# A two-layer graph kernel: the second product with U21 moved into the first step, diffusion tiles and exponentials put ahead of each group's first transposes

## The reference, cut to what matters

```python
h = maximum(layernorm(x), 0);  x = x + L0(h, adj)        # quantised support, then adj @ support
X = maximum(layernorm(x), 0)
R = (S + I) / rowsum(S + I);  Z = 0;  Xf = Xa = X        # S is adj
for s in range(2):
    A = adj_from_feats(Xa, W1, W2, W3)   # softmax(Xa W1 W2 (Xa W3)^T), the top 0.9 kept, softmax again
    Xf = R @ Xf
    Xa = A @ Xa
    Z = Z + (Xf @ U1s[s] + Xa @ U2s[s])
Y = X + Z
return x + (layernorm(Y) * gamma + beta)
```

## Time and profile before

| | |
|---|---|
| median of 3 runs | 1463.36 us (1462.64 to 1469.3) |
| the profiled execution | 1465.6 us, its span 1463.8 us |
| layer 0, up to the first logits of step 0 | 0 to 353.2 us |
| step 0, up to the first logits of step 1 | 353.2 to 923.8 us |
| step 1 with the output | 923.8 to 1463.8 us |
| busy, share of the span | TensorE 85%, VectorE 76%, ScalarE 41%, GpSimd 20% |
| mean granted TensorE clock | 0.967 |

### The profile page before, as it was taken

How to read it: one execution, slowest core, us unless ns; L and a number is a source line. 1 busy time by engine, 2 the same in 40 slices (tenths; PEclk the granted TensorE clock), 3 DMA queues, 4 the chain that set the end, 5 groups by cost and what they waited for, 6 DMA issues and landing times.

```text
span 1463.8 us, 18743 instructions
## 1 busy us (share of the span) xinstructions
PE 1239.3 (85%) x6458; PEld 607.9 (42%) x6458; DVE 1113.8 (76%) x1880; ACT 600.1 (41%) x1129; POOL 291.1 (20%) x233
## 2 busy tenths in 40 slices
PE   0348999997699689999989899789799999999994
PEld 0123555553244245444545454234344444444442
DVE  6985777773699999269949900499899989879667
ACT  1332444444831244455454343760234364353331
POOL 3312343432122213011122111011101011011011
PEclk9888999999899899999999999989999999999998
DMA  6124455442134211121110140524421121120244
GB/s 209 57 86 169 178 190 188 179 161 90 44 118 143 86 49 66 42 75 51 37 65 30 32 157 30 194 72 146 127 66 58 37 94 43 38 72 30 97 153 175
DMA packets 57687, 143.95 MB, mean 98 GB/s; under 512 B 9664, under 2 KB 9664, under 8 KB 53248
## 3 DMA queue, kind: packets, MB, share of 16 engines
q1 hardware_dynamic: 57600, 142.91, 28.3%
HBM read 90.72 MB, written 52.17 MB: 98 GB/s over the span
## 4 chain that ended last, share of the span: by engine, by line
PE 63%; issue 15%; ACT 9%; DVE 6%; POOL 4%; DMA 4%; POOLq 0%; SPq 0%; DVEq 0%; ACTq 0%
PE AB L785 15%; PE UB L647 9%; PE AB L788 8%; PE RB L745 6%; PE AB L637 4%; PE AB L630 3%; PE TB L656 3%; PE XB L647 3%; PE RB L647 3%; PE RB L747 2%; ACT squares L972 2%; POOL RT L541 2%; PE LB L720 2%; DMA AD<-z_d 2%; DMA AD<-xu_d 1%
## 5 line engine op out<-in xcount | busy, mean ns | idle before, releaser
L1268 DVE SCALAR_TENSOR_TENSOR WS<-E,g 128x2048 bf16<-128x2048 f32 x128 | 313.7, 2501 | 4.9 <-ACT E L992 3.8
L785 PE MATMUL AB<-XR,turns 128*128 128x512 f16 x1024 | 242.1, 380 | 0.0
L745 PE MATMUL RB<-VR,turns 128*128 128x512 f16 x704 | 165.7, 388 | 23.2 <-DMA turns<-adj_parts 23.2
L1355 DVE TENSOR_REDUCE g<-E 128x1 f32<-128x2048 f32 x32 | 73.0, 2280 | 126.5 <-ACT E L965 126.5
L785 PEld LDWEIGHTS AB<-XR,turns 128*128 128x128 f16 x1024 | 100.0, 98 | 105.4 <-issue 0.7
L541 POOL TENSOR_TENSOR RT<-RT,AD 128x512 f32<-128x512 f32 x32 | 57.5, 1795 | 382.6 <-ACT RT L1004 382.6
L788 PE MATMUL AB<-XR,turns 128*128 128x512 f16 x512 | 131.5, 380 | 0.0
L1029 ACT ACTIVATE turns<-TB 128x512 f16<-128x512 f32 x128 | 75.3, 594 | 124.9 <-PE TB L662 124.8
L745 PEld LDWEIGHTS RB<-VR,turns 128*128 128x128 f16 x704 | 68.7, 100 | 105.8 <-DMA turns<-adj_parts 27.1
L647 PE MATMUL UB<-UW,XT 128*128 128x512 f16 x384 | 88.2, 380 | 27.4 <-ACT XT L917 27.2
L965 ACT ACTIVATE E<-LB 128x512 f32<-128x512 f32 x128 | 75.4, 596 | 40.1 <-PE LB L721 38.0
(11 more groups left out here) (266 smaller groups left out, 2032.2 us busy)
## 6 DMA issues: line engine op xcount, KB each, us to landing
turns<-adj_parts SPq DMA_DIRECT2D x64, 512.0 KB, 3.8
E<-adjT SPq DMA_DIRECT2D x16, 1024.0 KB, 5.1
adj_parts<-turns SPq DMA_DIRECT2D x16, 1024.0 KB, 3.9
z_d<-UO SPq DMA_DIRECT2D x31, 256.0 KB, 2.0
XR<-x SPq DMA_DIRECT2D x4, 1024.0 KB, 12.0
WS<-U SPq DMA_DIRECT2D x4, 1024.0 KB, 5.3
x_d<-E SPq DMA_DIRECT2D x16, 256.0 KB, 2.6
xu_d<-UO SPq DMA_DIRECT2D x16, 256.0 KB, 2.0
```

The source lines that it names most:

```text
L745: i = mm(bank[:, :], AT[:, 0, j, :], VR[:, j, k % 2, :], start=(k == 0), stop=False)
L785: mm(AB[:, :], ET[:, 0, j, :], XR[:, j, y_, :], start=(j == 0 and y_ == 0), stop=False)
L1268: return v.scalar_tensor_tensor(junk[t % 2], e, g4[:, k, t:t + 1], e, op, ALU.mult, accum_out=g4[:, F_, t:t + 1])
```

## The change

- **U21 moves to step 0.** A X U21 with A of step 1 is A (X U21): after each tile of step 0, `w_product` multiplies the tile's X with U21 (12 matmuls into XB), and its halves W are stored to `x_parts` in X's place (GpSimd's lo half, `post`). In step 1 `terms_product` gives the finished sum, which `a_out` scales straight into UO: no transposes, splitting or product per tile. U21 has a buffer of its own (UV), is not stored and loaded, and `s_u21out` is gone.
- **W packed once.** W1·W2 and W3 are 64 columns each of one 128-column operand; `pk_product` is 12 matmuls instead of 24. ScalarE copies the result by five instructions instead of three, because the halves go to other partitions. VectorE prepares WPK with 4 instructions instead of 8.
- **Layer 0's transposes.** `x_halves_turned` transposes X's two float16 halves out of XR (8 transposes) four matmuls into the lo half of the next tile; it waits for `s_xl`, GpSimd's lo half of X. ScalarE copies both halves out at once (1024 columns). `x_turned`, `x_rest` and two copies go; the wait for `s_xT` on VectorE goes.
- **The tail of a tile in step 0 (`post`) is put into the next tile**, or, for a group's last tile, into the first diffusion tile of the next group; after group 3 `last_post` does it alone.
- **The banks AB and RB alternate** over diffusion tiles and attention tiles (`bank_of`, `bank_free`).
- **Diffusion tiles 9 to 15** are whole: one ahead of group 0, two ahead of groups 1, 2 and 3 (R_BEHIND = (1, 2, 2, 2)). The hi half of adj has a second buffer (AH), and SP loads it two tiles ahead (`r_done`).
- **`group_start`**: on ScalarE the order is the post of the last tile, the first diffusion tile's copy, the four exponentials of the next group (now those of group 1 too), the second diffusion tile's copy, and `e_hi` of chunks 0 and 1; on TensorE the diffusion tiles come first, then `e_turned` 0 and 1.
- The program is built with `dynamic_dma_scratch_size=1024`.

```diff
+R_FIRST = 9
+R_BEHIND = (1, 2, 2, 2)
...
-        def step_order(s, logits, terms, r_tile, r_tiles, pairs, r_behind):
+        def step_order(s, logits, terms, r_tile, r_tiles, group_start, pairs, last_post):
             logits(s, 0)
             terms(s, 0)
             r_tile(s)
             logits(s, 1)
-            r_tiles(s, 1, R_EARLY)
-            terms(s, 1)
-            r_tiles(s, R_EARLY, R_FIRST)
+            r_tiles(s, 1, R_FIRST)
             for g in range(NG):
-                if 0 < g < NG - 1:
-                    terms(s, g + 1)
-                if g < R_BEHIND:
-                    r_behind(s, R_FIRST + g * (1 + G // 2))
+                group_start(s, g)
                 pairs(s, g)
+            if s == 0:
+                last_post()
...
+            def r_done(s, t, odd):
+                if not isinstance(t, int) or t + 2 < T:
+                    at_hi_in(s, t + 2, odd)
+                if not isinstance(t, int) or t + 1 < T:
+                    at_lo_in(s, t + 1)
+                    ad_in(s, t + 1)
+                r_store(s, t)
...
+            def post(t):
+                pool.wait_ge(s_wf, t + 1 + OPEN)
+                pool.wait_ge(s_wh, t + 1)
+                q.tensor_tensor(XHL[:, 1, :], WF[:, :], XHL[:, 0, :], ALU.subtract).then_inc(s_wl, 1)
+                pk_lo(t + T, 1, t, s_wl, t + 1 - OPEN)
...
-                    if j == T // 2 and n is not None:
-                        x_rest(n)
+                    if j == T // 4 and n is not None:
+                        x_halves_turned(n)
                     mm(AB[:, :], turns[:, h, 1, j, :], sup[:, j, :], start=False, stop=(j == T - 1))
...
+            def x_halves_turned(n):
+                pe.wait_ge(s_pkc, n + OPEN)
+                pe.wait_ge(s_xh, n + 1)
+                pe.wait_ge(s_xl, n + 1 + OPEN)
+                for h in range(2):
+                    for k in range(KC):
+                        c = h * KC + k
+                        i = tr(XB[:, :].bitcast(F16)[:, c * P:(c + 1) * P],
+                               XR[:, bass.ds(n, 1), h, k * P:(k + 1) * P].rearrange("p o d -> p (o d)"), ident[:, :])
+                i.then_inc(s_xT, 1)
...
-                for w in range(2):
-                    i = three(XB[:, w * P:(w + 1) * P], lambda k: WPK[:, k, w, 0, :], lambda k: WPK[:, k, w, 1, :], xh, xl)
-                i.then_inc(s_pk, 1)
+                three(bank[:, 0:P], lambda k: WPK[:, k, 0, :], lambda k: WPK[:, k, 1, :], xh, xl).then_inc(s_pk, 1)
...
             def tile(s, g, i):
...
+                bank_free(s, first_use(g) + c)
+                terms_product(qq, 0, bank)
+                e_rest(qq, 2)
+                e_turned(qq, slot, 3)
+                if post:
+                    x_turned(t - 1 + T)
...
+                terms_product(qq, 1, bank)
+                e_rest(qq, 3)
+                if more:
+                    e_turned(qq + 1, after, 0)
+                if post:
+                    x_rest(t - 1 + T)
+                terms_product(qq, 2, bank)
+                if post:
+                    u_product(t - 1)
...
+                if post:
+                    w_product(t - 1)
...
+                terms_product(qq, 3, bank)
...
+                if post:
+                    p_and_k(t - 1)
...
+            def group_start(s, g):
+                t, count = G * g, R_BEHIND[g]
+                if s == 0 and g:
+                    xT_hi(t - 1 + T)
+                    xT_lo(t - 1 + T)
+                    post_out(t - 1)
+                    w_out(t - 1)
+                    pk(t - 1 + T, 1, t - 1, UB)
+                if g:
+                    r_out(s, first_r(g), bank_of(g, 0))
+                if g < NG - 1:
+                    terms(s, g + 1)
+                r_out(s, first_r(g) + count - 1, bank_of(g, count - 1))
+                e_hi(t + s * T, 0)
+                e_hi(t + s * T, 1)
```

More of the change, by code:

```diff
@@ L44, with first_use, first_r @@
 OPEN = 1
-R_GROUPS = 2
-R_BEHIND = 3
-R_FIRST = T - R_GROUPS * (G // 2) - R_BEHIND
-R_EARLY = R_FIRST - 2
 RUN = 4
+R_FIRST = 9
+R_BEHIND = (1, 2, 2, 2)
 R_HI = 2 * T
 R_ALL = R_HI + T
-R_CUTS = (0, 4, 17, 24, 28, 41, R_ALL)
+def first_use(g):
+    return R_FIRST + sum(R_BEHIND[:g]) + g * G
+def first_r(g):
+    return R_FIRST + sum(R_BEHIND[:g])
+BANK_USES = [("r", t) for t in range(R_FIRST)]
+for _g in range(NG):
+    BANK_USES += [("r", first_r(_g) + j) for j in range(R_BEHIND[_g])] + [("a", G * _g + i) for i in range(G)]
 class Chain:
@@ L111, in build @@
         UW = sb("UW", [P, KC, 2, D], F16)
[L112 removed]
+        UV = sb("UV", [P, KC, 2, D], F16)
+        AH = sb("AH", [P, T, P], F16)
+        WPK = sb("WPK", [P, KC, 2, P], F16)
         gb = sb("gb", [P, 2, D], F32)
@@ L385, in fin_out, with stores @@
                 sp.dma_start(out[slice(*FIN[b])].rearrange("t p d -> p t d"), y).then_inc(s_out, 16)
-            def tile(s, t, h, r, more):
-                if s == 0:
-                    x_store(t + T, t)
-                if h == 1 and r is not None:
-                    if more:
-                        at_lo_in(s, r + 1)
-                        ad_in(s, r + 1)
-                    r_store(s, r)
-                if s == 0:
-                    z0_store(t)
-                else:
-                    z_in(t)
-                    if t < T - 1:
-                        y_store(t)
-                if h == 0 and r is not None and more:
-                    at_hi_in(s, r + 1)
+            def stores(t):
+                x_store(t)
+                z0_store(t)
+            def group_start(s, g):
+                if s == 0 and g:
+                    stores(G * g - 1)
+                for j in range(R_BEHIND[g]):
+                    r = first_r(g) + j
+                    r_done(s, r, r % 2)
             def pairs(s, g):
@@ L418, in pairs @@
                 for i in range(G):
-                    r = r_of(g, i // 2)
-                    tile(s, g * G + i, i % 2, r, r is not None and r + 1 < T)
+                    t = g * G + i
+                    if s == 0:
+                        if i:
+                            stores(t - 1)
+                    else:
+                        z_in(t)
+                        if t < T - 1:
+                            y_store(t)
                     if last and i == 1:
@@ L881, in _ @@
+            step_order(0, logits, nothing, r_tile, r_tiles, group_start, pairs, last_post)
+            step_order(1, logits, nothing, r_tile, r_tiles, group_start, pairs, last_post)
         @block.scalar
@@ L1084, in tile @@
-                xT_hi(n)
-                if first:
-                    e_lo(qq + 1, 2)
-                    e_hi(qq + 1, 3)
-                if ahead:
-                    squared(qq + 2 * G, slot)
-                xT_lo(n)
-                if more:
-                    e_lo(qq + 1, 3)
-                r = r_of(g, i // 2)
-                if i % 2 and r is not None:
-                    r_out(s, r)
-                act.wait_ge(s_u, n + 1)
-                if s == 0:
-                    act.wait_ge(s_uout, 16 * n + OPEN)
-                else:
-                    act.wait_ge(s_uout, 32 * T + OPEN)
-                    act.wait_ge(s_yout, 16 * t + OPEN)
```

430 lines of the change are left out of this document (210 added, 220 removed).

## The result

The changed kernel takes 1477.04 us (median of 6 runs, 1475.53 to 1481.79) against 1465.66 for the kernel before beside it: a ratio of 1.0091, 95% interval [1.0071, 1.011]. The ratio is not the quotient of the two medians (1.0078): one of the six executions of the kernel before was slow, 1607.07 us, and is left out of the ratio, but not of its median. The change is small, but its interval lies above 1. The forecast was 1444 and the range ended at 1464, so both were wrong, and so was the sign. The profiled execution took 1475.58 us, its span is 1473.8; before, the span was 1463.8. Both spans are cut at the same two points, the first logits of step 0 and the first logits of step 1 (L and X in the prediction).

The account below looks back on a forecast made before the run. VectorE also paces layer 0, TensorE bounds step 0 and VectorE step 1. From the profiled 1465.6 us, +27 (layer 0), −21 (step 0) and −25 (step 1) give 1446.6; less 2.2, 1444 us, range 1420 to 1464.

Parts of the forecast that it names:

- Layer 0, +27 forecast: Layer 0: 27 us dearer, tiles 16.2 against 14.42 us, as the new transposes wait for GpSimd's lo half of X.
- eight add 0.45: Layer 0's lo half: eight float16 transposes add 0.45 us a tile, at the packed W's 0.056 us pitch.
- Step 0, −21 forecast: Step 0: 21 us cheaper, 549.5 us against 570.6, as TensorE's waits for adj's halves and X's copies go.
- a start-up of 1.5 per group: Step 0's group starts: 1.5 us allowed for each of four groups, 6 us in the sum.
- In step 0 that costs nothing: Step 0: `e_hi` and the second diffusion tile's copy queue behind ScalarE's exponentials at no cost, as VectorE ends in time.
- Step 1, −25 forecast: Step 1 and output: 25 us cheaper, 515 against 540, through earlier exponentials for groups 2 and 3 and a shorter end.
- The final 2.2 us: Whole kernel: 2.2 us taken off the sum of 1446.6, since the median lay that much below the profiled execution.
- (a): Rival, layer 0: the transposes don't stall, GpSimd's lo half coming by 11.3; 1422 us, chance 0.17.
- (c): Rival, layer 0: float16 transposes cost their single time, 0.263 us each, not the pitch; 1469 us, chance 0.08.
- (b): Rival, both steps: start-ups and ScalarE's order bring waits back, SP's order holds the end; 14 us more, 1458, chance 0.15.
- (d): Rival, both steps: VectorE's search is the bound, so the steps together gain only some 15 us; 1475 us, chance 0.07.
- The chance for slower, 0.11: Whole kernel: chance 0.11 that the change makes it slower, made up of (d) and some of (c).

Follow-up runs that it names:

- a_late: Changed kernel with layer 0's eight float16 transposes 12 matmuls into the lo half instead of 4; 1450.5 us, ratio 0.9916 to the kernel before.
- f_early: Changed kernel with ScalarE's and GpSimd's halves of X made first in layer 0's tiles, transposes ahead of the lo half; 1433.9 us, ratio 0.978.
- d_ehi: Changed kernel with, in step 0, `e_hi` ahead of the float16 copy of a group's last diffusion tile on ScalarE; 1463.3 us, ratio 1.0005.
- g_early_ehi: Changed kernel with the edits of f_early and d_ehi together; 1416.7 us, ratio 0.9666 to the kernel before.
- j_all: g_early_ehi with, at step 0's group starts, 12 diffusion matmuls ahead of the last X's transposes; 1412.0 us, ratio 0.9642 to the kernel before.
- h_exps_late: Changed kernel with step 1's exponentials of groups 2 and 3 behind the second tile of the group before; 1494.7 us, ratio 1.0198.
- c_double: Changed kernel with layer 0's eight float16 transposes done twice at the same place; 1485.8 us, ratio 1.0174 to the kernel before.
- l_filled: Changed kernel with six unread matmuls in TensorE's wait ahead of layer 0's transposes; 1475.6 us, ratio 1.006 to the kernel before.
- b_xlo_first: Changed kernel with GpSimd making X's lo half ahead of P's and K's in layer 0; 1457.2 us, ratio 0.996 to the kernel before.

## Why the prediction was wrong, step by step

**Layer 0, +27 forecast, +37.7 measured.** The mechanism was right: the wait, its cause (GpSimd's order), its end at 12.62, L513's 2.4 us. Mis-sized was the term "eight add 0.45": they added 0.93. The pitch was nearly right (0.060 against 0.056), but a burst has a fixed cost of another 0.45, which the row of four could not show: its 0.39 is the time to the end of the last transpose, not to the next matmul; (16.72 − 16.2) x 14 = 7 us. Left out altogether was the clock behind idle time: 4.2 us in the tiles, and 1.8 at the end, where after a wait of 4.83 us twelve matmuls take 4.59 instead of 2.76. Against that the start came 2.9 us earlier (first hand-over at 112.2 instead of 115.1), not 1.3. Neither number is shown to be the WPK instructions' worth: a_late and f_early, with the same prologue, have that hand-over at 116.2 and 116.7. The 275 ns that the Trainium skill gives for one (TensorE: Matmul & The Clock Gate, section "Part 4: PE-mode transpose") is not the price of each in a row: eight took 0.93 us, eight more 0.48.

**Step 0, −21 forecast, −0.6 measured.** The loop of diffusion tiles ended at L + 140.9 (141.5 forecast), a tile of groups 0 and 1 took 21.63 us (21.65), the last tail 12.3 (14.3). What failed is "a start-up of 1.5 per group" and with it "In step 0 that costs nothing". From the end of tile 9, the four transposes of each group's last X begin 87.1, 116.1, 108.0 and 105.7 us apart; the forecast's pieces are 81.2, 108.9, 101.9 and 101.9, so 6.0, 7.2, 6.1 and 3.8 are missing, 23 in all. The text did name the second diffusion tile's copy beside `e_hi` behind the exponentials, but asked only whether the exponentials were done in time. They were. It did not follow the copy's own chain: copy to RT, GpSimd's sum, copy to VHL, and only then `e_hi`, with TensorE idle in the meantime and at the lower clock after it. The pairs of d_ehi (19.0) and g_early_ehi (18.6) show that this was about 19 of the 23. The wait for XF at the starts, 3.0 us in three, was overlooked as well; with it gone j_all's trace is 3.6 us shorter there. With the two the account closes to about a us.

**Step 1, −25 forecast, −27.1 measured:** right, and by its reasons. The groups end where forecast to within 2.3 us, and h_exps_late shows that the exponentials' start sets them beyond some 10 us of slack. The final 2.2 us, taken off because the median lay below the profiled execution, rested on three executions; over six the median is 1465.66, level with it.

**The rivals.** (a), no stall, did not happen, but a_late and f_early show what it would have been worth. (Its own terms take off 23.5 us, 27 less 3.5, where it has 22.) (c), each transpose at 0.263, is refuted by c_double. (b) had the right stage and even names `e_hi`, but a price of 14 for what was 21, and that came mostly from one cause. (d) gave 1475, next to the result, for the wrong reason: VectorE was not the bound of step 0, as d_ehi shows. That it is next to the result is luck. The chance for slower, 0.11, left too little for two stages missing on the same side, layer 0 by 10.7 us and step 0 by 20.5.

## What to carry to other kernels

Where a change puts a new waiting instruction into an engine's queue, follow the whole chain of what stands ahead of it on the producing engine, with that chain's own waits on a third engine, and not only whether the largest item is done. Idle times of TensorE can cost more than they last: add the matmuls behind them at the lower clock, and expect that part to differ from run to run. What an engine waits for can sometimes be made earlier by reordering a few lines on the engine that makes it; here such reorders, with the same instructions, decided between 0.9% slower and 3.6% faster. And compare a stage of two profiles only where what stands ahead of the edit took the same time in both.

## What was unexpected of the hardware

- Eight float16 transposes of 128 columns inside a matmul stream cost 0.93 us and sixteen 1.41, so 0.06 us each and 0.45 us once. With the 1.42 us wait before them filled but for some 0.3 us it was 0.96 (l_filled), with no wait at all 0.80 (a_late).
- Two idle times of TensorE of 1.1 and 1.4 us, 1.0 us of work apart, were followed by a granted clock of 0.66 in a stretch of every third tile; with the second filled by useless matmuls the clock stayed at 1.00. With one of 0.9 (a_late), or with 1.1 and 0.2 (b_xlo_first), the granted clock was 1.00 in every tile of the one profile taken.
- The same program, profiled twice, had its longer tiles one tile apart, and kernels with the same layer 0 lost between 3.9 and 11.3 us in this way. From the first logits of step 0 to the first diffusion tile it took 13.6 or 16.1 us, at a granted clock of 0.89 or 0.52 over the first 13.5 us, also for the same program.
- VectorE's L1271 holds up whichever GpSimd instruction begins beside it: 2.38 us for 64 x 128 elements (0.42 otherwise), 2.68 for 128 x 512 (1.15 otherwise). The rule of the Trainium skill (SBUF — State Buffer, section "Who interferes with whom") stands up here in both orders, and the other way round: VectorE's L1282 takes 1.27 us where it begins 0.03 us after GpSimd's L505 (1.15), 0.51 in b_xlo_first, where it begins 0.07 us after the shorter L515 (0.42), and 0.29 ahead of the loop, beside neither.
